# Layer 1 of a two-layer attention and feed-forward kernel: the null key's weights join the softmax sums on VectorE

## The reference, cut to what matters

```
xn, cn = _ln(x, ln1_s, ln1_b), _ln(context, lnc_s, lnc_b)
q, (k, v) = xn @ Wq, split(cn @ Wkv)                 # 16 heads of 64
k = concatenate((nk, k)); v = concatenate((nv, v))   # the null key and value
attn = softmax(where(mfull, q * scale @ k.T, max_neg))
out = _ln((attn @ v) @ Wo, lno_s, lno_b)
# feed-forward, with rounded activations and weights:
y = bitlinear(silu(bitlinear(x, w_gate)) * bitlinear(x, w_up), w_down)
```

## Time and profile before

| | |
|---|---|
| median of 3 runs | 816.92 us (814.83 to 818.94) |
| profiled execution | 815.57 us, span 813.8 us, mean granted TensorE clock 0.985 |
| busy, share of the span | TensorE 94%, weight loads 80%, VectorE 81%, ScalarE 54%, GpSimd 59% |
| chain that ended last, by engine | TensorE 79%, VectorE 8%, DMA 4%, no releaser 3% |
| layer 1's loop | 32 iterations, from about 318 us to 789 us |

### The profile page before, as it was taken

How to read it: one execution, slowest core, us unless ns; L and a number is a source line. 1 busy time by engine, 2 the same in 40 slices (tenths; PEclk the granted TensorE clock), 3 DMA queues, 4 the chain that set the end, 5 groups by cost and what they waited for, 6 DMA issues and landing times.

```text
span 813.8 us, 28927 instructions
## 1 busy us (share of the span) xinstructions
PE 767.1 (94%) x10907; PEld 648.9 (80%) x10937; DVE 661.9 (81%) x1747; ACT 441.4 (54%) x1078; POOL 478.2 (59%) x912
## 2 busy tenths in 40 slices
PE   8999999998799998999999999999999999999973
PEld 6777777776598996888888888888888888888851
DVE  5888989877756665579889898898888988988866
ACT  4666667656065674445555555555545555555432
POOL 7767678887866773344554555545555465453424
PEclk9999999999999999999999999999999999999996
DMA  8986220000421211121121121221212213122110
GB/s 245 373 340 257 103 87 15 16 21 28 140 75 54 60 50 37 39 64 44 46 84 45 56 76 46 76 55 56 76 45 76 56 46 86 46 63 59 39 43 14
DMA packets 68253, 65.82 MB, mean 81 GB/s; under 512 B 23714, under 2 KB 49042, under 8 KB 68114
## 3 DMA queue, kind: packets, MB, share of 16 engines
q1 hardware_dynamic: 53250, 39.71, 17.3%
q10 hardware_dynamic: 12816, 20.06, 6.7%
q0 software_dynamic: 2048, 4.20, 1.7%
HBM read 35.89 MB, written 24.37 MB: 74 GB/s over the span
## 4 chain that ended last, share of the span: by engine, by line
PE 79%; DVE 8%; DMA 4%; issue 3%; POOL 2%; ACT 1%; SPq 1%; DVEq 0%; ACTq 0%; another core or an unknown queue 0%; POOLq 0%
PE psum L1905 7%; PE psum L1871 6%; PE psum L1792 6%; PE psum L1839 6%; PE psum L1819 6%; PE psum L1804 6%; PE psum L1039 4%; PE psum L432 4%; PE psum L421 4%; PE psum L414 3%; PE psum L1027 3%; PE psum L1916 3%; PE psum L403 2%; PE psum L1892 2%; PE psum L1861 2%
## 5 line engine op out<-in xcount | busy, mean ns | idle before, releaser
L2084 ACT ACTIVATE a_pT<-psum 128x512 f32<-128x512 f32 x128 | 69.5, 594 | 52.2 <-PE psum L1892 34.3
L720 DVE TENSOR_REDUCE l_mx<-psum 128x4 bf16<-128x512 f32 x128 | 81.9, 681 | 3.5 <-PE psum L403 1.9
L1572 POOL TENSOR_TENSOR f_hd<-f_hmc,a_wmean 128x1 f32<-128x1 f32 x32 | 6.7, 210 | 124.6 <-DVE f_hr L2323 123.4
L2227 DVE TENSOR_REDUCE a_mxf<-psum 128x8 f32<-128x1024 f32 x64 | 77.5, 1211 | 2.5 <-PE psum L1861 2.5
L1792 PEld LDWEIGHTS psum<-a_xT,a_Wq 128*128 128x128 f32 x512 | 64.4, 192 | 15.4 <-issue 13.9
L1804 PEld LDWEIGHTS psum<-a_cTm,a_Wk 128*128 128x128 f32 x512 | 64.3, 192 | 13.9 <-issue 13.9
L552 ACT ACTIVATE l_pT<-psum 128x512 f32<-128x512 f32 x128 | 70.5, 597 | 8.2 <-PE psum L421 7.9
L1566 POOL TENSOR_SCALAR f_hq<-f_ht 128x512 bf16<-128x512 f32 x31 | 60.3, 1946 | 20.0 <-ACT f_ht L2127 19.9
L1871 PE MATMUL psum<-a_qT,a_kT 64*128 64x128 f32 x1024 | 71.7, 280 | 0.0
L1839 PE MATMUL psum<-a_Wv,a_cTm 128*128 128x512 f32 x128 | 70.7, 638 | 0.1
L1792 PE MATMUL psum<-a_xT,a_Wq 128*128 128x128 f32 x512 | 69.6, 279 | 0.5 <-ACT a_xT L2067 0.5
(11 more groups left out here) (315 smaller groups left out, 2085.3 us busy)
## 6 DMA issues: line engine op xcount, KB each, us to landing
sorted_x<-r_zeros ACTq DMA_DIRECT2D x12, 1408.0 KB, 7.0
a_r_all<-a_r_rows SPq DMA_DIRECT2D x124, 128.0 KB
e_xt<-sorted_x SPq DMA_DIRECT2D x39, 64.0 KB, 1.8
sorted_y<-e_yt ACTq DMA_DIRECT2D x39, 64.0 KB, 1.6
e_w<-in_E_W1b SPq DMA_DIRECT2D x1, 2064.0 KB
a_cin<-in_ctx SPq DMA_DIRECT2D x32, 64.0 KB, 2.5
out<-f_x SPq DMA_DIRECT2D x32, 64.0 KB, 2.0
x_res<-in_x SPq DMA_DIRECT2D x1, 512.0 KB, 4.9
```

What stands on the lines that cost most here:

```text
L720: nc.vector.tensor_reduce(mx[:, s, Q4 * k:Q4 * k + Q4], maxp[k % 2].rearrange("p (h t) -> p h t", h=Q4), AX_X, ALU.max).then_inc(mx_ready, 1)
L2084: nc.scalar.activation(pT[:, 2 * half + e, :], tp[e], ACT.Exp, scale=SCALE).then_inc(exp_ready, 1)
L2227: nc.vector.tensor_reduce(mxf[:, 8 * half:8 * half + 8].rearrange("p (e h) -> p e h", e=2), psum[:, 0:2, :].rearrange("p e (h t) -> p e h ...
```

## The change

The null product goes. The clamp of the maxima now writes each head's maximum 8 times, so that after the transpose all 8 partitions of a head hold it, and `pnT` has the null weights on the same partitions as the sums; for that the heads' order on the partitions changes (half and pair swap places in `sel`, in `sums` and in the reciprocals' layout). VectorE adds `pnT` to `denP` into a new tile `denT` in SBUF, signals `den_ready`, and takes the reciprocal from `denT`. The next maximum scores (second half) and the next null exponential wait for `den_ready` instead of the reciprocal and the sums. The setup no longer makes `null_rows`.

In the last iteration the down product of block 27 moves from behind the gate to behind the up product, and into the bank `pb`; its `finish` on VectorE moves from behind the maxima to behind `h_range`. The waits that guard the banks follow.

```diff
-    down_of = [pa if f in (H_LAST - 1, LAST + 2) else pb for f in range(B)]
+    down_of = [pa if f == LAST + 2 else pb for f in range(B)]
...
-                    rows = r_rows.rearrange("(a e i) q -> a e (i q)", a=2, e=2)[half, e]
+                    rows = r_rows.rearrange("(e a i) q -> a e (i q)", a=2, e=2)[half, e]
...
-                first = 2 * 16 * half
-                nc.vector.tensor_tensor(sel[:, half, :], ident[:, first:first + Q4], ident[:, HD + first:HD + first + Q4], ALU.add)
-                for e in range(2):
-                    nc.vector.tensor_copy(null_rows[:, half, e, :, :],
-                                          ident[:, HD * e + first:HD * e + first + Q4].unsqueeze(2).broadcast_to([P, Q4, G]))
+                first, width = Q4 * G * half, Q4 * G
+                nc.vector.tensor_tensor(sel[:, half, :], ident[:, first:first + width:G], ident[:, HD + first:HD + first + width:G], ALU.add)
...
         def values(b, half):
-                pe.wait_ge(x4_ready, H_LAST)
+                pe.wait_ge(o_stats, 3 * (b - 2) + 1)
...
         def max_scores(b, half):
             if half == 1:
-                wait(pe, inverse_seq, b)
+                wait(pe, den_ready, b)
...
         def sums(b):
             if b < 4:
                 pe.wait_ge(sel_ready, b + 1)
-                pe.wait_ge(pn_ready, b + 1)
             pe.wait_ge(mxf_ready, 4 * b + 5 if b + 1 < B else 4 * b + 3)
             for i in range(Q4):
                 for j in range(Q4):
-                    nc.tensor.matmul(denP[32 * j:32 * j + 32, :], mask_sel[:, b % 2, i, :], pT[:, j, i * S:(i + 1) * S],
-                                     start=(i == 0), stop=False, skip_group_check=True)
-            nc.tensor.matmul(denP, null_rows[:].rearrange("p h e i g -> p (h e i g)"), pnT[:],
-                             start=False, stop=True, skip_group_check=True).then_inc(sums_done, 1)
+                    row = 32 * (2 * (j % 2) + j // 2)
+                    last = nc.tensor.matmul(denP[row:row + 32, :], mask_sel[:, b % 2, i, :], pT[:, j, i * S:(i + 1) * S],
+                                            start=(i == 0), stop=(i == Q4 - 1), skip_group_check=True)
+            last.then_inc(sums_done, 1)
...
         def down(f):
-                    pe.wait_ge(o_stats, 3 * (f + 2) + 1)
+                    pe.wait_ge(gt_ready, f + 2)
...
-            if not more:
-                down(b - 4)
             minus_max(b, 1)
             scores(b, 1)
...
                 up_part(f)
+            if not more:
+                down(b - 4)
             weighted(b, 0)
...
         def null_exp(b):
-            wait(act, sums_done, b)
+            wait(act, den_ready, b)
...
-            nc.vector.tensor_scalar(mx[:, b % 2, :, 32 * half:32 * half + Q4], mxf[:, 8 * half:8 * half + 8].rearrange("p (e i) -> p e i", e=2),
+            nc.vector.tensor_scalar(mx[:, b % 2, :, 32 * half:32 * half + 32].rearrange("p e (i g) -> p e i g", g=G),
+                                    mxf[:, 8 * half:8 * half + 8].rearrange("p (e i) -> p e i", e=2).unsqueeze(3).broadcast_to([P, 2, Q4, G]),
                                     0.0, None, ALU.max).then_inc(mx_ready, 1)
...
         def inverse(b):
             dve.wait_ge(sums_done, b + 1)
+            dve.wait_ge(pn_ready, b + 1)
+            nc.vector.tensor_tensor(denT[:], denP, pnT[:], ALU.add).then_inc(den_ready, 1)
+            dve.wait_ge(den_ready, b + 1)
             if b >= 1:
                 dve.wait_ge(r_stored, 16 * b)
-            nc.vector.reciprocal(rT[:], denP).then_inc(inverse_seq, 1)
+            nc.vector.reciprocal(rT[:], denT[:]).then_inc(inverse_seq, 1)
...
             maxima(b, 1)
             if b >= 5:
                 finish(b - 5)
-            if not more:
-                finish(b - 4)
...
                 h_range(f)
+            if not more:
+                finish(b - 4)
             if b >= 2:
                 quantise_x(b - 2)
             inverse(b)
```

More of the change, by code:

```diff
@@ L1310, in attention_ffn_block @@
     lift, lift_col, null_out = sb("lift", [P, 1]), sb("lift_col", [P, 1]), sb("null_out", [P, D])
-    null_rows = sb("null_rows", [P, 2, 2, Q4, G])
     s1, b1, sc_, bc = sb("s1", [P, 1]), sb("b1", [P, 1]), sb("sc", [P, 1]), sb("bc", [P, 1])
@@ L1328, in attention_ffn_block @@
     pT = sb("pT", [P, 4, Q4 * S])
-    pnT, rT = sb("pnT", [P, S]), sb("rT", [P, S])
+    pnT, denT, rT = sb("pnT", [P, S]), sb("denT", [P, S]), sb("rT", [P, S])
     r_all = sb("r_all", [P, 2, Q4 * S])
@@ L1363, in attention_ffn_block @@
     t_done, exp_ready, pn_ready = sem("t_done"), sem("exp_ready"), sem("pn_ready")
-    pv_done, sums_done, inverse_seq = (sem(n) for n in ("pv_done", "sums_done", "inverse_seq"))
+    pv_done, sums_done, den_ready, inverse_seq = (sem(n) for n in ("pv_done", "sums_done", "den_ready", "inverse_seq"))
     r_stored, r_spread = sem("r_stored"), [sem(f"r_spread{half}") for half in range(2)]
@@ L1925, in spread_reciprocals @@
                 for e in range(2):
-                    h_ = 8 * half + 4 * e + i
+                    h_ = 8 * e + 4 * half + i
                     last = nc.tensor.matmul(r_bank[half][e * HD:(e + 1) * HD, i * S:(i + 1) * S],
```

## The result

The changed kernel takes 811.66 us (median of 7 runs, 808.32 to 814.06) beside 818.75 for the kernel before on the same chip: ratio 0.9925, interval 0.9900 to 0.9949. A second set gave 812.79 beside 818.14, ratio 0.9917 (0.9888 to 0.9946). It is faster, by under 1%: some 6 to 7 us by these ratios, 7.1 and 5.4 by the medians, where 9.6 were forecast for the profiled execution. 811.66 lies 5 us above the forecast time, above the 805 to 809 that were given for the forecast itself and inside the wider range, 802.5 to 812.5. The profiled execution took 811.33 us, with a span of 809.6 and a granted clock of 0.985 as before.

A forecast was written before the change was run, and what follows sets the result against it. TensorE sets the loop's pace, VectorE having under a microsecond to spare. 30 iterations x 0.22 = 6.6 us plus 3.0 in the last iteration give 9.6 off, forecast 806.6 us (805 to 809; wider 802.5 to 812.5).

The forecast's parts named there:

- The null product: TensorE in layer 1's loop: dropping it saves 0.22 us per iteration, 6.6 over 30; the 0.10 shape change stays.
- rival A: TensorE in the loop: the shape change's 0.10 goes too, 0.32 us per iteration, so 804 us; chance 0.12.
- VectorE's additions: VectorE in the loop: sum 0.33 and two clamps 0.04 each, +0.41 us per iteration, which just fits the new period.
- rival B: Loop: VectorE takes the pace, period 14.6 to 14.68 us, so 810 to 812 us; chance 0.17.
- Rival C: Loop: GpSimd holds up the reciprocal reading SBUF by 0.36 to 0.75 us, so 818.5 to 830 us; chance 0.08.
- The wait of the maximum scores: TensorE in the loop: waiting for the sum alone takes 0.95 us off, covering the reciprocal's 0.33 us later end.
- The reciprocals' way to the weighted values: Store and four loads by SP in layer 1 start 0.33 us later; no cost booked, nor any second-iteration gain.
- The last iteration: Moving the down product behind the up product saves 3.0 us, between 2.8 by VectorE and 3.4 by TensorE.
- neither is late: Last iteration: the moved down product's DMA (by 778.2) and VectorE's gate multiply (tanh ends 777.5) are there in time.
- Without the stand I expect 2.4 GHz throughout: Last iteration: scores and values run at full clock once TensorE no longer stands for the DMA, 0.7 + 0.9 us.
- The forecast's base: Median of the runs of the kernel before, 816.92 us, 1.35 above the profiled execution; less 9.6 it gives 807.3.

The follow-up runs named there:

- hidden_before: Kernel before, with TensorE's sums ahead of the weighted products and VectorE's next maxima ahead of the normalise: 825.00 us, ratio 1.0114.
- wait_recip: Changed kernel, with the next maximum scores waiting for the reciprocal again instead of the sum: 812.75 us, ratio 0.9933 to the kernel before.
- const_recip: Changed kernel, normalising all blocks but the last by a constant tile, store and loads still running: 807.76 us, ratio 0.9902 to the kernel before.
- hidden: Changed kernel, with TensorE's sums ahead of the weighted products and VectorE's next maxima ahead of the normalise: 809.70 us, again 806.69 (0.9896, 0.9864 to the kernel before).
- const_before: Kernel before, with all layer 1 blocks but the last normalised by a constant tile, store and loads still running: 815.69 us, ratio 0.9975.
- tail_only: Kernel before, with only the last iteration's down product and its finish moved: 816.64 us, ratio 1.0003.
- shift: Changed kernel, with 276 long-met waits (138 instructions) at the start of TensorE's program, moving its code against the fetch packets: 820.44 us in one execution.
- null_only: Changed kernel, with the last iteration's down product and finish left where they were: 816.30 us, ratio 0.9984 to the kernel before.
- fetch_more: Changed kernel, with 128 more long-met waits at the end of each SP iteration from the fifth on: 817.85 us, ratio 1.0008 to the kernel before.
- merged: Changed kernel, with two loads over 128 partitions in place of the four that spread the reciprocals: 1040.85 us, ratio 1.2754 to the kernel before.

## Why the prediction was wrong in its size

**The null product: right.** Period 14.49 against 14.50; rival A (0.32 per iteration) is out. The 0.10 of the shape change stayed: the first keys' group reads 1.16 instead of 1.06. hidden_before shows the same price at three places. The Trainium skill (TensorEngine Tiling (Array Packing), Key Properties) says that a change of the tiling mode drains TensorE; the trace agrees, with 0.10 to 0.11 us at each such place.

**VectorE's additions: right.** Sum 0.28, reciprocal 0.95, clamps 0.20 in the median and 0.38 at most (0.17 and 0.27 before), wait for the output product gone. In the regular iterations TensorE does not wait for the finished block, so rival B is not what happened, though VectorE's pace did come in by another loop. Rival C (GpSimd delays the reciprocal) is out: 0.95 as before.

**The wait of the maximum scores: overrated.** I wrote that with the old wait "TensorE would, with a period 0.22 shorter, reach it first"; it does, by 0.02 us at most (wait_recip).

**The step that failed: "The reciprocals' way to the weighted values, a store and four loads by SP, starts 0.33 later; in the whole layer one load was waited for, 0.72 us in the second iteration ... I book no gain for that iteration."** I took the absence of waits for room and did not work out this loop, as I had done for the values. The reading was short too: behind late stores the kernel before waits up to 0.27 us ahead of the second half of the normalise, which the timeline marks "issue". The cover fell from 8.1 to 7.5 us, and VectorE's 0.61 of idle time, which had made such waits good, went into the added work. In after a wait of 0.46 to 0.65 makes the next period 0.37 to 0.66 longer.

That is 2.87 and 3.48 us of late periods, of the 6.6 booked. They have two sources. Every fourth or fifth store comes 0.5 to 1.6 us late; behind such stores lie 1.33 and 0.66 of the late time. The larger part, 1.54 and 2.82, lies in seven iterations whose store is punctual (1.68 to 1.69 us) and whose loads land late, as at 537.42 above. const_recip takes the wait away and has the whole gain of the loop; hidden gives it room and has it too; const_before shows that there was next to nothing to win there before the change.

**The last iteration: right in size in part by luck, wrong in "neither is late".** tail_only's profile gives 3.23 us (3.0 forecast), shift 3.45. But of the 3.4 by which up was to come sooner, 1.6 stood on "Without the stand I expect 2.4 GHz throughout", and const_before has 2.4 GHz with the stand; against its 15.95, tail_only gains 1.66. And in after the down product, now due sooner, stands again. TensorE's timeline there, against the earlier trace rows:

```profile
776.17 0.39 PE L1950 MATMUL psum<-f_wq,f_xqT 128*128 128x512 bf16 x1 [0.68 <-ACT a_v L2109]
777.58 0.40 PE L1974 MATMUL psum<-f_wq,f_hqT 128*128 128x128 bf16 x4 [1.02 <-DMA f_hqT<-f_hq]
777.91 3.31 PE L1901 MATMUL psum<-a_pT,a_v 128*32 128x128 f32 x64
```

The transposing DMA, issued behind the four loads, landed 4.83 us after its issue, where before it took 2.9 (issued at 775.22, and the down product starts at 778.20), and the normalise waited 1.91 us for its loads; a 16 KB packet began 6.6 us after the reciprocal. The weighted sums then took 3.31 us, as in null_only, at a granted clock of 0.50 (778.4 to 781.6); in the second profile of after the clock stayed at 1.00 and they took 1.95. So last and then are 0.14 us better than before in the first profile and 2.32 in the second. In tail_only and shift no such packet ran there, and the gain is whole; hidden had one and its down product stood 0.31 and 0.06 us.

Together: of 9.6 forecast, the two profiles of after have 3.75 and 5.65. Missing are 3.0 and 3.3 in the loop and 2.9 and 0.7 at its end. The forecast's base, 816.92, was also a little below the 817.0 to 818.8 that before took beside the others.

Open: what makes the loads late, the larger part of the late time, was only seen, not tried. In the two profiles of after, all seven iterations with a punctual store and a wait have a 16 KB packet that started 4.1 to 5.0 us behind the loads' issue; ten more with such a packet have no wait, and the 19 without one have none either. Open too is why the clock falls behind a stand in one execution and not in another.

## What to carry to other kernels

Where no wait shows, ask how much room there is: follow every loop that passes through a DMA once around, from the end of the producer to the use, and compare with the new period. A saving on the bound engine shortens the cover of every such round trip, and work put ahead of the producer shortens it again. Then ask what idle time the engine that would wait has left, since that makes a small wait good. The remedy may be order alone: start the producer sooner, and move other work between the transfer and its use.

## What the runs showed of the hardware

**Instruction code delays small transfers.** TensorE's code comes in packets of 16 KB on a queue of its own (86 in after, for 21,716 recorded products and weight loads, about 253 each; 138 instructions of TensorE more in shift made it 87, while fetch_more, which adds to SP's code, kept 86). In twelve of the profiles (all but merged and fetch_more) there are 372 stores of 8 KB by SP: with no such packet starting between 0.2 us ahead of the reciprocal's end and 1.75 us behind it, 264 stores took at most 1.80 us; with one starting 0.2 to 1.25 us behind it, all 72 took 2.28 to 3.83 (the other 36, with one just outside that, 1.7 to 3.7). shift moved the packets and the late stores with them. An 8 KB packet of the other instruction queue did no such harm in the same place (before, b = 16: store 1.73). The Trainium skill (Runtime: NRT & Kernel Launch, Instruction fetch mechanics) says that code is streamed in 16 KiB blocks of 256 instructions and that this is mostly hidden. The count of the trace agrees. Hidden it was from TensorE (in const_recip every period from b = 4 to 29 is 14.49, packet or not), but not from the data transfers beside it.

**A load whose pattern has an outer dimension of 2** (merged, with the broadcast in the middle of the pattern) ran on some two of the 16 DMA engines: busy 0.13, 52 GB/s, against 0.52 and 156 GB/s for the four loads of after. VectorE stood 202.9 us for the reciprocals' loads, against 8.4 in after.

**The same stand does not always bring the clock down.** Behind a stand of 2.57 us ahead of the down product TensorE's granted clock fell to 1.2 GHz in before (0.50 from 779.1 to 782.3), and behind 2.63 us in const_before it stayed at 2.4 (1.00 from 774 to 784).
